# A Mamba-style block with a mixture of experts on one core: inner products kept by a ScalarE copy, without VectorE's mask product

## The reference

```python
zxbcdt = x @ Win.T
z, xBC, dt = split(zxbcdt)                   # 256, 512 and 4 columns
xBC = silu(causal_conv4(xBC) + conv_b)       # x_ssm (256), B (128), C (128)
dtp = softplus(dt + dt_bias)
dA  = exp(dtp * A)                           # one decay for each of 4 heads
# scan over the tokens t of a sequence:
h = dA_t * h + (dt_t * x_t) B_t^T
y = C_t . h + D * x_t
y = rmsnorm(y) * norm_w * silu(z)
x = layernorm(x + y @ Wout.T)
```

## Time and profile before

| | us |
|---|---|
| median of 3 runs | 737.92 |
| lowest and highest | 737.48, 739.69 |
| the profiled execution, its time | 741.33 |
| the profiled execution, its span from first to last instruction | 739.5 |
| mean granted TensorE clock in it | 0.967 |
| the 16 slots | about 36 to 430 of the span |
| the experts | about 430 to the end |

### The profile page before, as it was taken

The page is one execution under the profiler, slowest core; times in us unless marked ns, Lnnn a source line. Parts: engine busy times, 40 slices in busy tenths (PEclk is TensorE's granted clock), DMA queues, the critical chain, the costliest instruction groups (busy, mean ns, idle before and its releaser), DMA issues.

```text
span 739.5 us, 19955 instructions
## 1 busy us (share of the span) xinstructions
PE 661.4 (89%) x5075; PEld 542.4 (73%) x5075; DVE 565.0 (76%) x1874; ACT 474.7 (64%) x1176; POOL 454.2 (61%) x648
## 2 busy tenths in 40 slices
PE   7978999999999999999998889999999999989800
PEld 5846766676666766676666579999999999988800
DVE  3388899989999999999999667667666667776644
ACT  3746767776687767676776437756655665666625
POOL 5023277777777777677776656767765555666643
PEclk9999999999999999999999799999999999999955
DMA  9180001110111011101110132333432224546243
GB/s 253 34 285 15 5 30 30 40 45 19 36 35 44 20 41 32 43 23 37 33 41 19 29 72 63 92 85 96 99 82 67 78 70 119 150 143 178 78 158 129
DMA packets 56399, 54.54 MB, mean 74 GB/s; under 512 B 9546, under 2 KB 45518, under 8 KB 56032
## 3 DMA queue, kind: packets, MB, share of 16 engines
q1 hardware_dynamic: 44704, 32.10, 16.4%
q0 software_dynamic: 8416, 16.93, 6.8%
q10 hardware_dynamic: 3168, 4.22, 1.6%
HBM read 31.05 MB, written 22.63 MB: 73 GB/s over the span
## 4 chain that ended last, share of the span: by engine, by line
PE 71%; DVE 11%; issue 9%; POOL 3%; DVEq 2%; ACT 2%; DMA 2%; SPq 0%; POOLq 0%; ACTq 0%
PE p L607 12%; PE pl L598 8%; PE pj L460 6%; PE p L598 4%; PE p L689 4%; PE p L659 4%; PE p L653 4%; PE p L697 3%; PE p L635 3%; PE pj L468 2%; PE p L668 2%; PE p L571 2%; PE p L557 2%; PE p L468 2%; PE pl L504 2%
## 5 line engine op out<-in xcount | busy, mean ns | idle before, releaser
L1634 POOL DMA_INDIRECT moe_rows<-xT x135 | 134.2, 994 | 91.2 <-DVE xT L1250 59.0
L1567 POOL DMA_INDIRECT sorted_rows<-pair,slot x128 | 128.7, 1006 | 32.5 <-issue 31.3
L1008 DVE SCALAR_TENSOR_TENSOR acc<-pj,conv_w_sb,acc 128x511 f32<-128x511 f32 (+2 forms) x192 | 142.4, 742 | 4.1 <-ACT acc L792 1.1
L607 PE MATMUL p<-w,xT 128*128 x1080 | 143.9, 276 | 1.8 <-DVE xT L1246 1.7
L927 ACT ACTIVATE xT<-pl,b_sb 128x128 f32<-128x128 f32 x360 | 103.1, 370 | 50.0 <-PE pl L598 48.4
L607 PEld LDWEIGHTS p<-w,xT 128*128 128x128 f32 x1080 | 132.0, 193 | 2.3 <-issue 2.2
L598 PE MATMUL pl<-xT 128*128 128x128 f32 x720 | 96.8, 278 | 2.4 <-DVE xT L1238 2.4
L598 PEld LDWEIGHTS pl<-xT 128*128 128x128 f32 x720 | 88.5, 194 | 3.1 <-issue 2.5
L1246 DVE TENSOR_TENSOR xT<-p,b_sb 128x128 f32<-128x128 f32 x135 | 39.1, 290 | 61.8 <-PE p L607 53.9
L792 ACT ACTIVATE acc<-pj,conv_b_sb,conv_w_sb 128x512 f32<-128x512 f32 x64 | 49.5, 773 | 33.5 <-PE pj L460 33.4
L927 ACT ACTIVATE xT<-p,b_sb 128x128 f32<-128x128 f32 x180 | 51.5, 370 | 25.1 <-PE p L598 24.1
(11 more groups left out here) (217 smaller groups left out, 1420.9 us busy)
## 6 DMA issues: line engine op xcount, KB each, us to landing
xT<-sorted_rows SPq DMA_DIRECT2D x135, 65.0 KB, 1.9
xres<-in_x SPq DMA_DIRECT2D x16, 256.0 KB, 3.1
w<-in_w SPq DMA_DIRECT2D x2, 2048.0 KB, 10.0
acc<-moe_rows SPq DMA_DIRECT2D x16, 256.0 KB, 4.0
xc<-moe_rows SPq DMA_DIRECT2D x16, 256.0 KB
out<-sz ACTq DMA_DIRECT2D x16, 256.0 KB, 2.4
moe_rows<-xT POOLq DMA_INDIRECT x135, 2.5
sorted_rows<-pair,slot POOLq DMA_INDIRECT x128, 2.6
```

The lines of the kernel that those rows point to most:

```text
L607: mm = pe.matmul(y_bank(j)[:, 0:P], hT[j % 4][:, f, :], w2[:, bass.ds(e, 1), f, :].rearrange("p e d -> p (e d)"), start=(f == 0), stop=(f ...
L1008: ins = dve.scalar_tensor_tensor(out=acc[:, k, j:TOKS], in0=pj[k % 2][:, 0:TOKS - j], scalar=conv_w[:, k, TAPS - 1 - j:TAPS - j], in1=acc[ ...
L1567: pool.indirect_dma_start(out=sorted_rows[:, :], out_offset=bass.IndirectOffsetOnAxis(slot[q.par][:, c, k:k + 1], 0), in_=(rowA, rowB)[k][ ...
L1634: pool.indirect_dma_start(out=moe_rows[:, :], out_offset=bass.IndirectOffsetOnAxis(xs[k][:, P:P + 1].bitcast(I32), 0), in_=ye[j % 8], in_o ...
```

## The change

ScalarE gets a new step, `keep_products`: a plain copy of the bank `p7` into `Gm`, between the two Silu of z, in the prologue and in each slot that prepares a next sequence. It waits for the inner products (`G_psum`) and for VectorE's last use of the old `Gm` (`M_ready`). VectorE's product with `upto` at the start of each scanning slot is gone, and with it its wait for `G_psum`; `Gm_ready` is now raised by ScalarE. What lies below the diagonal in `Gm` is no longer zeroed there; the decays that it is multiplied with are zero at these places.

```diff
+            def keep_products(q):
+                act.wait_ge(G_psum, q.n + 1)
+                wait(act, M_ready, NC * q.n)
+                act.copy(Gm[:, :, :], p7[:, :].rearrange("p (c k) -> p c k", c=NC)).then_inc(Gm_ready, 1)
+
...
-                for k in range(CC):
-                    gate_part(q, k)
+                gate_part(q, 0)
+                keep_products(q)
+                gate_part(q, 1)
...
@@ slot_dve @@
                 if scan:
                     dve.wait_ge(cur_ready, s.n + 1)
-                    dve.wait_ge(G_psum, s.n + 1)
-                    dve.tensor_tensor(Gm[:, :, :], p7[:, :].rearrange("p (c k) -> p c k", c=NC),
-                                      upto[:, :].unsqueeze(1).broadcast_to([P, NC, P]),
-                                      ALU.mult).then_inc(Gm_ready, 1)
-                if scan:
                     mask_chunk(s, 0)
```

## The result

| | before | after |
|---|---|---|
| first comparison, median of 5 runs each (us) | 739.59 | 742.78 |
| lowest and highest | 737.48, 739.78 | 741.83, 743.75 |
| profiled execution: time, span | 741.33, 739.5 | 742.78, 740.9 |
| its mean granted TensorE clock | 0.967 | 0.967 |

What follows compares the result with a forecast made beforehand. The prediction took the chain along TensorE, ScalarE's `Btok` and VectorE's `Xdt` as the bound, with VectorE idle 0.57 us there. Terms 0 + 0 + 0 left the median of 737.92, forecast 737.9 us, range 736.4 to 740.0.

Steps and rivals of the forecast that it cites:

- Middle slots, 14 x 0: At 14 middle slot boundaries, `Xdt` stays held by `Btok`, which waits for TensorE; removed product and added copy change 0 us.
- First slot, 0 within 0 to +0.45: In the first slot the second Silu falls behind the copy; `Btok` moves by 0, at worst 0.45 us late.
- Last slot, 0: In the last slot `Xdt` comes at most 0.09 us earlier, lost again before TensorE's next work; bounds -0.09 to 0.
- The sum: Over the whole kernel, the terms 0 + 0 + 0 with bounds -0.1 and +0.5: no change, chance 0.87.
- The clock rival: TensorE's low clock at 410.0 to 421.3 goes away (733.5 us) or a second drop comes (742.3); chance 0.02 each.

Runs made afterwards that it cites:

- a4_add_only: Kernel before plus a ScalarE copy of 128x512 (of xT, into a spare tile) between the two Silu of z; VectorE keeps its product: median 739.15, ratio 1.0000.
- b1_padded: Changed kernel with a VectorE memset of 4 columns in place of each of the 16 products left out: median 739.17, ratio 1.0002 to the kernel before.
- d1_before_pad_front: Kernel before with 15 small memsets added in VectorE's prologue and no work moved: median 739.96, ratio 1.0009.
- c1_middle_only: Kernel before with the change in slots 1 to 14 alone, first and last slot in the old form: median 740.35, ratio 1.0013.
- c2_ends_only: Kernel before with the change in the first and last slots alone, slots 1 to 14 in the old form: median 739.66, ratio 1.0005.
- b3_pad_front: Changed kernel with 15 small memsets added together in VectorE's prologue: median 741.89, ratio 1.0029 to the kernel before.

## Why the prediction was wrong, point by point

- **Middle slots, 14 x 0: right as a statement on the moved work.** The copy took 0.565 to 0.587 us, 16 times, against 0.57 taken from the earlier trace rows; no table load came; `Btok` still waits for the transposes at all 14 boundaries. In a4_add_only a copy of this size at this place cost nothing that could be measured.
- **First slot, 0 within 0 to +0.45: right**, with -0.01. **Last slot, 0: right**, with the 0.08 earlier `Xdt` (0.09 was forecast) lost again ahead of TensorE's next wait.
- **The sum was wrong, and the step that failed is its premise**, that the cost of the change is the cost of the instructions moved and of the waits next to them. Taking 16 instructions out of VectorE's queue also shifts everything behind them against the places in its order at which the queue stops for 0.2 to 0.5 us. Before, the two stops of the profiled execution (0.30 at 88.50 and 0.34 at 379.11) fell ahead of idle time. After, they fell on pieces of VectorE's work for which TensorE waits: +0.78 us (the 0.08 and 0.07 of slots 10 and 13 are put down to stops as well, of 0.05 and 0.18; only the two large ones were followed). That the stops hang on the place in the queue and not on the moved work is seen in the traces from both sides: b1_padded keeps all the moved work and the two large stops are gone, d1_before_pad_front moves no work and has about +1.0 in its distances. In the times it shows only at equal clock (0.26 and 1.41 on the line); the ratios of both hold 1.000 in their intervals. The trace of before held the hint, a row with 0.34 us idle and "issue" behind it, between instructions that wait for nothing; the prediction doesn't mention it.
- **The clock rival was dismissed too lightly.** It had 0.02 on the slower side, because "nothing shows" that small shifts would do anything to the clock. It didn't need a shift of mine: the long drop in the last slot comes and goes between executions of one program, and so does the one in the first slot. Low mean clocks are 43 of 126 before and 20 of 29 after. The median of low executions is 740.11 before against 738.56 for the others, and 741.80 against 738.81 after. A straight line through all 155 executions, time against mean clock, with one offset for the changed kernel, gives 0.28 us for each 0.001 of clock and an offset of 1.31 (standard error 0.12). The mean clocks, 0.9727 and 0.9707, are 0.0020 apart. So about 0.57 of the 1.87 goes with the clock and 1.31 doesn't. The line describes these executions; it doesn't say what the clock would give back.
- **What stays open.** Of the 1.31 the traces show 0.78 as stops; the rest, about 0.5, wasn't found in any slot. On the same line b1_padded lies 0.26 above the kernel before with +0.42 in its trace, c1_middle_only 0.45 with +0.15, c2_ends_only 0.74 with nothing in the middle slots, and b3_pad_front 2.06 with +0.83. So the stops don't account for every difference. The later start of the first slot, from 38.33 to 39.72 us, is one thing that differs between executions and stands in no distance; whether it has a part in this the 17 traces are too few to say. Why the changed kernel falls into the long drop twice as often isn't settled: neither the ends alone (5 of 12) nor the middle alone (7 of 12) is far enough from 43 of 126 to say, and b1_padded, with the time of before, had 6 of 12. In the first comparison all five executions after had a mean clock between 0.965 and 0.969, which accounts for a part of its 0.53%; in the next 24 executions this was so for 9. Even on the line these five lie 2.02 above the kernel before and the next 24 only 1.16; why isn't known.
- **The range was too narrow** whatever the mechanism. It took its spread from three runs, the highest at 739.69, and treated the profiled execution, at 741.33, as beside the matter. That one was ordinary: later executions of the kernel before lie between 737.2 and 741.9. With the bounds of its terms right, the range would still have missed the later medians after, 741.14 and 741.07.

## What to carry to other kernels

A sum over moved instructions can be right at every place and the kernel still differ by 0.1% to 0.3%, in part because a queue that is longer or shorter has its stops elsewhere. Where a forecast says 0, keep that much on either side, and look in the trace for stops of 0.2 to 0.5 us marked "issue": what idle time covers them now, and what would stand there after so many instructions more or less. When two kernels are this close, compare mean clocks before times, and repeat the comparison before explaining it. Here one memset of 4 columns in each slot moved two stops off the chain, worth 0.6 us, and brought two others worth 0.4, while 16 products of 128x512 taken from an engine that was 91% busy gave back nothing.

## What the runs showed of the hardware that was not expected

- VectorE's queue stopped for 0.18 to 0.46 us at places of its order that were the same in every trace of a program (four traces of the kernel before with and without fillers, five of the changed one), and an instruction packet of 8 KB began 0.57 to 0.71 us after such a stop (31 stops; once 0.97).
- The same program had a stretch at 1.2 GHz behind TensorE's waits in the last slot that was short in one execution (11.81 us between `Btok` and `Btok`, span 736.8) and long in another (13.04, span 739.5). It makes 1.2 of the 2.7 us between the two.
- A second stretch of low clock, 0.79 from 44 to 52 us, was there in six of 17 traces, of both kernels, and in just those whose first `Btok` came at 39.34 us or later; it made the first slot longer by 0.65 us in the trace after.
- Keeping TensorE busy through these gaps held the clock at 1.00 from 404 to 424 us, and cost 3.3 us net (742.45 against 739.15 in the means).
